# A graph network's fourth pass: scaling the node states on ScalarE instead of VectorE

## The chip, the cores and the metric

The kernel runs on one core of a Trainium2 chip. The metric is device time in microseconds for one launch, taken as the median of the runs shown. A core has five engines with an instruction stream each, which meet only at semaphores: TensorE (PE in the profile: matmuls and transposes), VectorE (DVE), ScalarE (ACT), GpSimd (POOL, which issues the indirect DMAs here) and SyncE (SP, which issues the plain ones). An engine takes its own instructions strictly in the order in which they were written.

## The reference

The network has 3125 nodes with 128 features and 100000 edges, sorted by destination. Four layers follow each other (a mean layer, three attention layers as one, a PNA layer, a SAGE layer), each after a layer norm. The change touches the end of the PNA layer only:

```python
msg = concat([node_feat[src], node_feat[dst]]) @ M_w.T + M_b
denom = maximum(deg, 1.0)[:, None]
mean = segment_sum(msg, dst) / denom
has_edge = (deg > 0)[:, None]
mx = where(has_edge, segment_max(msg, dst), 0.0)
mn = where(has_edge, segment_min(msg, dst), 0.0)
sq_mean = segment_sum(msg * msg, dst) / denom
std = sqrt(maximum(sq_mean - mean * mean, 0.0) + 1e-30)
h = concat([mean, mx, mn, std])
h = concat([h, h * amp, h * att])
h = (concat([node_feat, h]) @ U_w.T + U_b) * (1 / sqrt(n))
x = x + batch_norm(h)
```

Since `msg` is a part that depends on the source plus a part that depends on the destination, the kernel sums the source part alone and adds the destination's part (called `root`) to the mean, the largest and the smallest once for each node. The deviation does not need it.

## The kernel before

The 3125 nodes are 25 tiles of 128 nodes (`NT = 25`), the nodes on partitions and the features along the free dimension. At the end of a pass they are taken in five batches of five tiles (`NB = 5`, `BT = 5`).

The edges are walked in four passes, three for the attention layers and the fourth for PNA (`p.kind == PNA`). Each of 128 lanes walks 784 edges and stores a running state for every edge to DRAM (`rows`). For PNA that state has four blocks of 128 features: the sum of squares, the sum, the largest, and the largest of the negated values (so minus the smallest). After the last edge GpSimd fetches for each of the 25 tiles the state at each node's last edge (L645, one indirect DMA a tile) into `ends(p)`, which is a part of the large buffer `big`, as most tensors here.

Then come the steps that the change is about.

- **Node states.** A node whose edges begin in an earlier lane needs that lane's state. TensorE fetches it with a one-hot matmul for each tile (L1111, `psY<-Z,pick`, 128x512, f32, two banks in turn). VectorE's `node_states(b)` combines it: an add for the two sums (L1685) and a max for the two others (L1686), which raises `node_rdy`. TensorE's matmul of tile t waits for VectorE to have read tile t-2.
- **Layer out.** VectorE's `layer_out(b)` works on a whole batch, 128 x 640 elements for one block: the squares and the sum times `hrec` (one over the degree, or 0), the two largest times `has` (1 or 0), the mean squared into `mean_sq`, the subtraction, the max with 0 (L1730, raises `sd_in`), and `root` added to the three other blocks (L1731 to L1733, the last raises `agg_rdy`; the negated one turns over its sign there). That is ten instructions, L1724 to L1733.
- VectorE's order is `node_states(0)`, `node_states(1)`, `layer_out(0)`, `node_states(2)`, `layer_out(1)` and so on, then `layer_out(3)`, `layer_out(4)`.
- **ScalarE** takes the square root of a batch (L884, raises `sd_rdy`) and then copies the transposed tiles of that batch from PSUM (L889).
- **The product with U.** Once all 25 tiles have been combined, TensorE transposes four blocks of tile t (L1130, needs `agg_rdy` and `sd_rdy` of its batch), waits for ScalarE's copy (L889, `aggT_rdy`), and multiplies (L1141, eight instructions of 128x384 in the trace for a tile). Its order is: transposes of tile t, product of tile t-1, then two small matmuls that sum tile t-3 over the nodes (L1121). VectorE reads each product with three instructions (L1746 to L1748, raises `pna_rdy`); the product of tile t needs tile t-2 to have been read.

After the product come the batch norm, the layer norm, and the SAGE layer with dense adjacency counts (L934), which ends the kernel. TensorE works there almost without a gap.

Of the kernel before, what the change touches and what calls it, by code (L numbers as in the profile page):

```python
# [5 lines left out]
ALU = mybir.AluOpType  # L6
ACT = mybir.ActivationFunctionType
# [78 lines left out]
def build(nc, x, src, dst, W0, b0, Ws, Wd, att_s, att_d, gat_b, M_w, M_b, U_w, U_b, gamma, beta,  # L86
# [37 lines left out]
    with ExitStack() as ctx:  # L124
        def sb(name, shape, dt=F32):
            return ctx.enter_context(nc.sbuf_tensor(name, shape, dt))
# [4 lines left out]
        def sem(name):  # L131
            return ctx.enter_context(nc.semaphore(name))
# [42 lines left out]
        last = sb("last_s", [P, NT])  # L175
        has = sb("has", [P, NT])
        nohas = sb("nohas", [P, NT])
        hrec = sb("hrec", [P, NT])
# [122 lines left out]
        aggT = ring[:, NT * 4 * D:NT * 4 * D + 8 * P].rearrange("p (a w) -> p a w", a=2)  # L301
        mean_sq = ring[:, NT * 4 * D + 8 * P:NT * 4 * D + 8 * P + BT * D].rearrange("p (t d) -> p t d", d=D)
        rest = ring[:, NT * (TW + D):NT * (2 * TW + D)].rearrange("p (t w) -> p t w", w=TW)
        assert NT * (2 * TW + D) <= GMAX and NT * 4 * D + 8 * P + BT * D <= SIDE and NT * 4 * D <= ABUF

# [76 lines left out]
        sd_in, sd_rdy = sem("sd_in"), sem("sd_rdy")  # L382
        agg_rdy = sem("agg_rdy")
        aggT_ps, aggT_rdy = sem("aggT_ps"), sem("aggT_rdy")
# [266 lines left out]
        def _(act):  # L651
# [78 lines left out]
            for p in passes:  # L730
# [137 lines left out]
                if p.kind == GAT:  # L868
# [7 lines left out]
                    if g == 2:  # L876
                        deviations(2)
                        normalize(2)
                else:
                    for t in range(NT):  # L880
                        if t % BT == 0:
                            at = slice(t, t + BT)
                            act.wait_ge(sd_in, t // BT + 1)
                            nc.scalar.activation(ends(p)[:, at, 0:D], ends(p)[:, at, 0:D], ACT.Sqrt,  # L884
                                                 bias=eps[:, 1:2]).then_inc(sd_rdy, 1)
                        act.wait_ge(aggT_ps, t + 1)
                        if t >= 2:
                            act.wait_ge(pna_ps, t - 1)
                        nc.scalar.copy(aggT[:, t % 2, :], psT[t % 2][:]).then_inc(aggT_rdy, 1)  # L889
# [294 lines left out]
        def _(dve):  # L1184
# [270 lines left out]
            link(v.tensor_scalar(att[:], att[:], PNA_DELTA, None, ALU.mult))  # L1455
            link(v.tensor_scalar(amp[:], amp[:], 1.0 / PNA_DELTA, None, ALU.mult))
            dve.wait_ge(cross_ps, 1)
            link(v.tensor_scalar(cbias[:], psH[:, 0:NT], -1.0, BIG, ALU.add, ALU.mult))

            for p in passes:  # L1460
# [239 lines left out]
                def layer_out(b):  # L1700
# [21 lines left out]
                    else:  # L1722
                        sq, sm_, mx, nm = (e[:, :, k * D:(k + 1) * D] for k in range(4))
                        v.tensor_tensor(sq, sq, over_feats(hrec[:, at]), ALU.mult)  # L1724
                        link(v.tensor_tensor(sm_, sm_, over_feats(hrec[:, at]), ALU.mult))
                        v.tensor_tensor(mx, mx, over_feats(has[:, at]), ALU.mult)
                        link(v.tensor_tensor(mean_sq, sm_, sm_, ALU.mult))
                        v.tensor_tensor(nm, nm, over_feats(has[:, at]), ALU.mult)
                        link(v.tensor_tensor(sq, sq, mean_sq, ALU.subtract))
                        v.tensor_scalar(sq, sq, 0.0, None, ALU.max).then_inc(sd_in, 1)  # L1730
                        v.tensor_tensor(sm_, sm_, r_, ALU.add)  # L1731
                        link(v.tensor_tensor(mx, mx, r_, ALU.add))
                        v.tensor_tensor(nm, r_, nm, ALU.subtract).then_inc(agg_rdy, 1)  # L1733

# [68 lines left out]
```

## Time and profile before

| What | Value |
|---|---|
| median of 3 runs | 5279.04 us (5275.83 to 5281.31) |
| the profiled execution's own time | 5277.98 us |
| its span | 5275.9 us |
| node states and layer out of the fourth pass | 4765.0 to 4833.9 us |
| the product with U | its first tile at 4820.1, its last at 4908.7 us |
| SAGE layer's dense stage (L934) | from 4956.0 us to the end |

The profile is one execution. A row of the view of lines groups instructions of one form: busy time in total and the mean length of one, then the idle time of the engine just before them and what ended it. Busy time counts overlapped pieces once, so busy time divided by the count is the pace at which such instructions follow each other, and can be shorter than the mean length of one. A row of the timeline is one instruction or several merged ones: start, length, engine, line, the tiles; in brackets how long the engine had been idle and who ended that. A start and a length are in microseconds. The stretches' view gives busy time of each engine and the clock that TensorE was granted, where 1.00 is full speed, 2.4 GHz, and 0.50 is 1.2 GHz.

### The profile page before, as it was taken

What the parts mean: (1) busy time and instruction counts of PE and PEld (TensorE: products, weight loads), DVE (VectorE), ACT (ScalarE), POOL (GpSimd) and SP (SyncE); (2) the same over time, 40 slices, a digit from 0 to 9 for tenths busy, and PEclk for the clock granted to TensorE, in tenths of its full rate; (3) what the DMA queues carried; (4) which work ended last, traced back from release to release, by engine and by line L of the source; (5) the groups of instructions that cost most, each with busy time, mean ns of one, the idle gap of its engine ahead of it and who ended that gap; (6) DMA issues with size and microseconds to landing.
All of it is one profiled execution on the core that took longest, in us unless ns stands there. A gap on an engine that the chain in (4) does not pass through costs nothing.

```text
span 5275.9 us, 65740 instructions
## 1 busy us (share of the span) xinstructions
PE 3320.8 (63%) x13965; PEld 1555.5 (29%) x13965; DVE 4374.3 (83%) x14057; ACT 3173.8 (60%) x10162; POOL 3130.6 (59%) x3140
## 2 busy tenths in 40 slices
PE   4555578677777657777764777777343433336799
PEld 1111134333333233333322333333221111113444
DVE  7999989699999869999996999999788888885211
ACT  5666610677777557777764777777377777770100
POOL 3444400677777677777776777777377777771000
PEclk9999997788988778888886989898767667678899
DMA  4333362344444434444442444444267777772466
GB/s 140 131 131 131 131 246 95 86 128 128 127 122 129 120 82 129 127 123 127 129 123 68 128 129 129 123 126 129 60 244 278 281 280 282 280 279 64 177 234 224
DMA packets 324085, 817.57 MB, mean 155 GB/s; under 512 B 71032, under 2 KB 238948, under 8 KB 308904
## 3 DMA queue, kind: packets, MB, share of 16 engines
q1 hardware_dynamic: 225336, 605.05, 31.1%
q0 software_dynamic: 95024, 206.12, 16.4%
q10 hardware_dynamic: 3392, 2.75, 0.2%
q8 instruction: 112, 1.84, 0.1%
q14 instruction: 221, 1.81, 0.1%
HBM read 352.28 MB, written 461.40 MB: 154 GB/s over the span
## 4 chain that ended last, share of the span: by engine, by line
DVE 33%; POOL 18%; issue 11%; PE 11%; ACT 8%; DMA 6%; POOLq 0%; DVEq 0%; SPq 0%; ACTq 0%
POOL big L631 17%; DVE big L1606 8%; DVE big L1523 7%; PE psT L934 6%; DMA big<-table,src_win 4%; DVE big L1596 4%; DVE big L1546 2%; ACT hT L792 2%; DVE big L1616 2%; PE psY L1141 1%; DVE lane_x L1374 1%; DMA big<-A_d 1%; POOL big L645 1%; ACT hT L798 1%; ACT hT L807 1%
## 5 line engine op out<-in xcount | busy, mean ns | idle before, releaser
L631 POOL DMA_INDIRECT big<-table,src_win x2744 | 2647.8, 965 | 894.6 <-issue 798.6
L1054 PE MATMUL psY<-big,hT 128*128 128x420 bf16 x4200 | 1080.6, 405 | 725.0 <-ACT hT L798 724.1
L792 ACT ACTIVATE hT<-src_bc,node_c 128x128 bf16<-128x128 f16 x4200 | 1289.9, 386 | 63.2 <-DMA src_bc<-pe_src_d 54.2
L1606 DVE SCALAR_TENSOR_TENSOR big<-big,keep_win 128x132 f32<-128x132 f32 x2184 | 782.4, 358 | 77.8
L1054 PEld LDWEIGHTS psY<-big,hT 128*128 128x128 bf16 x4200 | 408.2, 110 | 1388.1 <-ACT hT L798 618.2
L1523 DVE TENSOR_SCALAR big<-src_bc,node_c 128x128 bf16<-128x128 f16 x4200 | 714.0, 284 | 0.6 <-issue 0.5
L1082 PE MATMUL psS<-big,hT 128*128 128x384 bf16 x1400 | 353.1, 430 | 549.4 <-DVE hT L1533 549.4
L798 ACT ACTIVATE hT<-hT 128x640 bf16<-128x640 bf16 x840 | 589.3, 720 | 0.0
L590 POOL TENSOR_SCALAR big<-big 128x400 bf16<-128x400 f16 x198 | 285.1, 1440 | 356.6 <-PE psY L993 166.8
L823 ACT ACTIVATE psH<-d_b 128x60 f32<-128x60 f32 x168 | 37.6, 224 | 695.2 <-DVE d_b L1588 695.2
L1060 PE MATMUL psL<-big 128*128 128x420 bf16 x2100 | 395.0, 344 | 18.1 <-DVE big L1523 15.6
L1060 PE MATMUL psZ<-big 128*128 128x420 bf16 x2100 | 390.0, 341 | 7.9 <-DVE big L1523 5.9
L1082 PEld LDWEIGHTS psS<-big,hT 128*128 128x128 bf16 x1400 | 170.3, 124 | 732.0 <-issue 694.1
L1596 DVE TENSOR_TENSOR big<-big,psH 128x1848 f32<-128x1848 f32 x168 | 349.4, 2080 | 26.2 <-ACT psH L823 22.1
L718 ACT ACTIVATE big<-big 128x400 bf16<-128x400 bf16 x396 | 212.3, 536 | 201.0 <-PE psY L993 99.4
L689 ACT COPY big<-psT 128x512 f32<-128x512 f32 (+1 forms) x21 | 11.3, 540 | 500.3 <-PE psT L934 500.3
L1295 DVE TENSOR_SCALAR big<-big 128x400 bf16<-128x400 f16 x990 | 306.8, 356 | 0.0
L934 PE MATMUL psT<-big 128*128 128x512 f32 (+1 forms) x700 | 281.2, 564 | 19.4 <-DMA big<-A_d 18.8
L1060 PEld LDWEIGHTS psL<-big 128*128 128x128 bf16 x2100 | 202.6, 98 | 208.3 <-DVE big L1523 37.6
L993 PE MATMUL psY<-big 128*128 128x400 bf16 x792 | 169.5, 337 | 144.0 <-DVE big L1295 144.0
L1060 PEld LDWEIGHTS psZ<-big 128*128 128x128 bf16 x2100 | 200.6, 98 | 195.4 <-DVE big L1523 29.6
L604 POOL DMA_INDIRECT start_ad<-big,start_i x75 | 81.2, 1082 | 282.3 <-ACT big L741 265.2
(327 smaller groups left out, 5381.8 us busy)
## 6 DMA issues: line engine op xcount, KB each, us to landing
rows<-big SPq DMA_DIRECT2D x112, 1792.0 KB
rows<-big SPq DMA_DIRECT2D x168, 952.0 KB
big<-A_d SPq DMA_DIRECT2D x18, 6400.0 KB, 19.8
A_d<-big SPq DMA_DIRECT2D x396, 200.0 KB, 1.9
big<-table,src_win POOLq DMA_INDIRECT x2744
src_bc<-pe_src_d SPq DMA_DIRECT2D x168, 64.0 KB
table<-big SPq DMA_DIRECT2D x15, 350.0 KB
big<-A_d SPq DMA_DIRECT2D x3, 1600.0 KB, 6.9
```

Of the source, the lines that this page charges most:

```text
L590: pool.tensor_scalar(hot_q[:, t % HOTS, GJ - 2, :], iota_q, qT[:, GJ - 2, t:t + 1], None, ALU.is_equal).then_inc(hot_p, 1)
L631: pool.indirect_dma_start(out=rows[:, k, 0:p.table_w], out_offset=None, in_=table, in_offset=bass.IndirectOffsetOnAxis(ap=src_win[:, s, k: ...
L792: ins = nc.scalar.activation(is_src[:, t, P:P + n], src_bc[:, s % 2, P:P + n], ACT.Square, bias=node_c[:, t:t + 1], scale=-1.0)
L798: nc.scalar.activation(is_src[:, at, 0:n], is_src[:, at, P:P + n], ACT.Relu, bias=1.0, scale=-1.0).then_inc(is_src_rdy, 1)
L934: ins = nc.tensor.matmul(psT[at % 2][:, 0:n * W].rearrange("f (b w) -> f b w", w=W), rows[:, s, :], abuf[(at + 1) % 2][:, 0:n, W * s:W * s ...
L1054: ins = nc.tensor.matmul(psF[0][s % 2][:, 0:3 * p.table_w], is_src[:, t, 0:P], table_s[:, t, :, :].rearrange("p c w -> p (c w)"), start=(t ...
L1060: ins = nc.tensor.matmul(psF[1][s % 2][:, 0:3 * p.table_w], is_src_v[s % 2][:, t, :], table_s[:, t, :, :].rearrange("p c w -> p (c w)"), s ...
L1082: ins = nc.tensor.matmul(psS[:, 0:3 * D].rearrange("p (c w) -> p c w", c=3), is_src[:, t, 0:P], table_s[:, t, :, 0:D], start=(n == 0), sto ...
L1295: ins = v.tensor_scalar(hot_q[:, t % HOTS, j, :], iota_q, qT[:, j, t:t + 1], None, ALU.is_equal)
L1523: ins = v.tensor_scalar(is_src_v[s % 2][:, t, :], src_bc[:, s % 2, 0:P], node_c[:, t:t + 1], None, ALU.is_equal)
L1596: v.tensor_tensor(for_heads, for_heads, over_heads(by_edge(cw_p[:, :, 1:15]), HC), ALU.mult).then_inc(chained, 1)
L1606: v.scalar_tensor_tensor(state[:, k, 0:GATW], prev[k][:, 0:GATW], kw[:, 0, k:k + 1], rows[:, k, 0:GATW], ALU.mult, ALU.add).then_inc(chain ...
```

## The change

ScalarE's stream at the end of the fourth pass gets the scaling. For each tile, as soon as VectorE has combined it, it multiplies the largest by `has`, the negated smallest by `minus` (a new tensor, minus `has`, so that the sign is turned here), and writes the square of the sum times `hrec` to `mean_sq`, of which there are now two buffers. After five tiles it multiplies the squares and the sum of each tile by `hrec` in one instruction of 128x256 in place, and raises `scaled`. Then it takes the square root of the batch before. VectorE's `layer_out` keeps three instructions: the subtraction, the max, and one add of `root` to the three other blocks at once (128 x 5 x 384). It waits for `scaled` first. The copies of the transposed tiles now come after all five square roots.

```diff
@@ ScalarE, end of the fourth pass
+                    en = ends(p)
+                    for b in range(NB + 1):
+                        for t in range(BT * b, min(BT * (b + 1), NT)):
+                            act.wait_ge(node_rdy, NT * p.number + t + 1)
+                            if t % BT == 0 and b >= 2:
+                                act.wait_ge(sd_in, b - 1)
+                            nc.scalar.mul(en[:, t, 2 * D:3 * D], en[:, t, 2 * D:3 * D], has[:, t:t + 1])
+                            nc.scalar.mul(en[:, t, 3 * D:4 * D], en[:, t, 3 * D:4 * D], minus[:, t:t + 1])
+                            nc.scalar.activation(mean_sq[b % 2][:, t % BT, :], en[:, t, D:2 * D], ACT.Square,
+                                                 scale=hrec[:, t:t + 1]).then_inc(squared, 1)
+                        if b < NB:
+                            act.wait_ge(squared, BT * (b + 1))
+                            for t in range(BT * b, BT * (b + 1)):
+                                ins = nc.scalar.mul(en[:, t, 0:2 * D], en[:, t, 0:2 * D], hrec[:, t:t + 1])
+                            ins.then_inc(scaled, 1)
+                        if b:
+                            at = slice(BT * (b - 1), BT * b)
+                            act.wait_ge(sd_in, b)
+                            nc.scalar.activation(en[:, at, 0:D], en[:, at, 0:D], ACT.Sqrt,
+                                                 bias=eps[:, 1:2]).then_inc(sd_rdy, 1)
                     for t in range(NT):
-                        if t % BT == 0:
-                            at = slice(t, t + BT)
-                            act.wait_ge(sd_in, t // BT + 1)
-                            nc.scalar.activation(ends(p)[:, at, 0:D], ends(p)[:, at, 0:D], ACT.Sqrt,
-                                                 bias=eps[:, 1:2]).then_inc(sd_rdy, 1)
                         act.wait_ge(aggT_ps, t + 1)
@@ VectorE, before the passes
+            link(v.tensor_scalar(minus[:], has[:], -1.0, None, ALU.mult))
@@ VectorE, layer_out
-                        sq, sm_, mx, nm = (e[:, :, k * D:(k + 1) * D] for k in range(4))
-                        v.tensor_tensor(sq, sq, over_feats(hrec[:, at]), ALU.mult)
-                        link(v.tensor_tensor(sm_, sm_, over_feats(hrec[:, at]), ALU.mult))
-                        v.tensor_tensor(mx, mx, over_feats(has[:, at]), ALU.mult)
-                        link(v.tensor_tensor(mean_sq, sm_, sm_, ALU.mult))
-                        v.tensor_tensor(nm, nm, over_feats(has[:, at]), ALU.mult)
-                        link(v.tensor_tensor(sq, sq, mean_sq, ALU.subtract))
+                        dve.wait_ge(scaled, b + 1)
+                        sq = e[:, :, 0:D]
+                        link(v.tensor_tensor(sq, sq, mean_sq[b % 2], ALU.subtract))
                         v.tensor_scalar(sq, sq, 0.0, None, ALU.max).then_inc(sd_in, 1)
-                        v.tensor_tensor(sm_, sm_, r_, ALU.add)
-                        link(v.tensor_tensor(mx, mx, r_, ALU.add))
-                        v.tensor_tensor(nm, r_, nm, ALU.subtract).then_inc(agg_rdy, 1)
+                        others = e[:, :, D:4 * D].rearrange("p t (k d) -> p t k d", d=D)
+                        v.tensor_tensor(others, others, r_.unsqueeze(2).broadcast_to([P, BT, 3, D]), ALU.add).then_inc(agg_rdy, 1)
```

VectorE's stream before, from the last tile of `node_states(1)` over `layer_out(0)` to the first tile of `node_states(2)`:

```order
L1686 SCALAR_TENSOR_TENSOR big<-psY,cbias,big 128x256
L1724 TENSOR_TENSOR big<-big,hrec 128x5x128 [waits node_rdy]
L1725 TENSOR_TENSOR big<-big,hrec 128x5x128
L1726 TENSOR_TENSOR big<-big,has 128x5x128 [waits dve_chain]
L1727 TENSOR_TENSOR big<-big 128x640
L1728 TENSOR_TENSOR big<-big,has 128x5x128 [waits dve_chain]
L1729 TENSOR_TENSOR big<-big 128x5x128
L1730 TENSOR_SCALAR big<-big 128x5x128 [waits dve_chain]
L1731 TENSOR_TENSOR big<-big 128x5x128
L1732 TENSOR_TENSOR big<-big 128x5x128
L1733 TENSOR_TENSOR big<-big 128x5x128 [waits dve_chain]
L1685 TENSOR_TENSOR big<-psY,big 128x256 [waits node_ps,ends_in2]
```

VectorE's stream of the change, the same `layer_out(0)` between the same neighbours:

```order
L1744 TENSOR_TENSOR big<-big 128x5x128 [waits scaled,node_rdy]
L1745 TENSOR_SCALAR big<-big 128x5x128 [waits dve_chain]
L1747 TENSOR_TENSOR big<-big 128x5x384
```

Seven of ten instructions are gone, and the first that is left waits for ScalarE.

ScalarE's stream before, from the last edge of the pass on:

```order
L839 ACTIVATE psH<-big 128x128
L884 ACTIVATE big<-big,eps 128x5x128 [waits sd_in]
L889 COPY big<-psT 128x512 [waits aggT_ps] x2
L889 COPY big<-psT 128x512 [waits pna_ps,aggT_ps] x3
L884 ACTIVATE big<-big,eps 128x5x128 [waits sd_in]
```

ScalarE's stream of the change in the middle of it: the last square of a batch, its five scalings, the square root of the batch before, and the next batch's first tile:

```order
L890 ACTIVATE big<-big,hrec 128x128
L895 ACTIVATE big<-big,hrec 128x256 [waits squared]
L895 ACTIVATE big<-big,hrec 128x256 x4
L900 ACTIVATE big<-big,eps 128x5x128 [waits sd_in]
L888 ACTIVATE big<-big,has 128x128 [waits sd_in,node_rdy]
L889 ACTIVATE big<-big,minus 128x128
```

And at its end, where both last square roots stand ahead of the first copy of a transposed tile:

```order
L895 ACTIVATE big<-big,hrec 128x256 x4
L900 ACTIVATE big<-big,eps 128x5x128 [waits sd_in] x2
L906 COPY big<-psT 128x512 [waits aggT_ps] x2
L906 COPY big<-psT 128x512 [waits pna_ps,aggT_ps] x23
```

ScalarE's first copy has moved from behind the first square root to behind the fifth. TensorE's stream is the same in both.

## Rows read from the trace of the kernel before

**Rows 1.** The page, part 1: busy time, share of the span, instructions of each engine.

```profile
PE 3320.8 (63%) x13965; PEld 1555.5 (29%) x13965; DVE 4374.3 (83%) x14057; ACT 3173.8 (60%) x10162; POOL 3130.6 (59%) x3140
```

**Rows 2.** Timeline, VectorE and ScalarE in the first layer out of the fourth pass.

```profile
4776.45 0.85 DVE L1724 TENSOR_TENSOR big<-big,hrec 128x640 f32<-128x640 f32 x1
...
4780.41 0.82 DVE L1729 TENSOR_TENSOR big<-big 128x640 f32<-128x640 f32 x1
...
4781.74 0.81 DVE L1731 TENSOR_TENSOR big<-big 128x640 f32<-128x640 f32 x1
4781.85 0.83 ACT L884 ACTIVATE big<-big,eps 128x640 f32<-128x640 f32 x1 [34.11 <-DVE big L1730]
...
4783.31 0.82 DVE L1733 TENSOR_TENSOR big<-big 128x640 f32<-128x640 f32 x1
...
4784.06 0.42 DVE L1685 TENSOR_TENSOR big<-psY,big 128x256 f32<-128x256 f32 x1
```

**Rows 3.** Timeline, node states of the second batch: VectorE's tiles 5 and 7, TensorE's last.

```profile
4771.53 0.42 DVE L1685 TENSOR_TENSOR big<-psY,big 128x256 f32<-128x256 f32 x1 [0.46 <-PE psY L1111]
...
4773.57 0.42 DVE L1685 TENSOR_TENSOR big<-psY,big 128x256 f32<-128x256 f32 x1 [0.46 <-PE psY L1111]
...
4776.47 0.30 PEld L1111 LDWEIGHTS psY<-Z,pick 128*128 128x128 f32 x2 [0.88 <-DVE big L1686]
```

**Rows 4.** Timeline, node states of the third and fifth batch, and TensorE's restart.

```profile
4784.92 7.08 PE L1111 MATMUL psY<-Z,pick 128*128 128x512 f32 x10 [7.32 <-DVE big L1686]
...
4790.85 0.82 DVE L1724 TENSOR_TENSOR big<-big,hrec 128x640 f32<-128x640 f32 x1
...
4812.45 0.42 DVE L1685 TENSOR_TENSOR big<-psY,big 128x256 f32<-128x256 f32 x1
...
4818.71 0.83 DVE L1724 TENSOR_TENSOR big<-big,hrec 128x640 f32<-128x640 f32 x1
```

**Rows 5.** Stretches: busy PE, PEld, DVE, ACT, POOL, TensorE's clock, DMA share, GB/s.

```profile
4770.00:4777.00 7.00, 6.70 (x14) 2.16 (x14) 5.60 (x14) 0.00 (x0) 5.28 (x6) 1.00 0.71 211
...
4785.00:4790.00 5.00, 5.00 (x7) 2.09 (x8) 2.22 (x6) 0.00 (x0) 2.84 (x3) 0.56 0.65 188
```

**Rows 6.** Timeline, the beginning of the product with U.

```profile
4818.73 1.09 PE L1130 MATMUL psT<-ident,big 128*128 128x128 f32 x8 [0.91 <-DVE big L1686]
...
4823.18 2.75 PE L1141 MATMUL psY<-wT,big 128*128 128x384 f32 x8
4823.38 0.59 ACT L889 COPY big<-psT 128x512 f32<-128x512 f32 x1 [2.89 <-PE psT L1130]
...
4834.98 5.49 PE L1141 MATMUL psY<-wT,big 128*128 128x384 f32 x8 [8.61 <-DVE big L1748]
...
4841.08 2.75 PE L1141 MATMUL psY<-wT,big 128*128 128x384 f32 x8
...
4844.32 2.75 PE L1141 MATMUL psY<-wT,big 128*128 128x384 f32 x8
```

**Rows 7.** Lines by form, ScalarE: busy us, mean ns of one, idle before.

```profile
L792 ACT ACTIVATE hT<-src_bc,node_c 128x128 bf16<-128x128 f16 x4200 | 1289.9, 386 | 63.2 <-DMA src_bc<-pe_src_d 54.2 <-PE psY L1054 9.0
...
L662 ACT ACTIVATE big<-xt,shift,rstd 128x128 f32<-128x128 f32 x100 | 38.9, 479 | 0.0
...
L884 ACT ACTIVATE big<-big,eps 128x640 f32<-128x640 f32 x5 | 4.1, 830 | 34.1 <-DVE big L1730 34.1
```

**Rows 8.** The page, part 5: VectorE's long multiplication with a broadcast operand.

```profile
L1596 DVE TENSOR_TENSOR big<-big,psH 128x1848 f32<-128x1848 f32 x168 | 349.4, 2080 | 26.2 <-ACT psH L823 22.1
```

**Rows 9.** Timeline of TensorE: one form (128x512, f32) after a shorter and a longer gap.

```profile
786.42 2.05 PE L1012 MATMUL psL<-sm,ones 128*128 128x512 f32 x2 [4.09 <-DVE tmp L1390]
...
856.23 1.10 PE L1012 MATMUL psL<-sm,ones 128*128 128x512 f32 x2 [3.38 <-DVE tmp L1390]
```

**Rows 10.** Timeline: GpSimd's last fetch of end rows that the timeline lists.

```profile
4787.76 0.94 POOL L645 DMA_INDIRECT big<-rows,end_i  x1 [0.30 <-issue]
```

**Rows 11.** Timeline: VectorE before the passes, the wait behind `minus`.

```profile
933.35 0.18 DVE L1458 TENSOR_SCALAR cbias<-psH 128x25 f32<-128x25 f32 x1 [5.06 <-PE psH L1025]
```

More of the change, by code:

```diff
@@ L176, in build @@
         has = sb("has", [P, NT])
+        minus = sb("minus", [P, NT])
         nohas = sb("nohas", [P, NT])
@@ L301, in build @@
         aggT = ring[:, NT * 4 * D:NT * 4 * D + 8 * P].rearrange("p (a w) -> p a w", a=2)
-        mean_sq = ring[:, NT * 4 * D + 8 * P:NT * 4 * D + 8 * P + BT * D].rearrange("p (t d) -> p t d", d=D)
+        mean_sq = [ring[:, NT * 4 * D + 8 * P + z * BT * D:NT * 4 * D + 8 * P + (z + 1) * BT * D].rearrange("p (t d) -> p t d", d=D)
+                   for z in range(2)]
         rest = ring[:, NT * (TW + D):NT * (2 * TW + D)].rearrange("p (t w) -> p t w", w=TW)
-        assert NT * (2 * TW + D) <= GMAX and NT * 4 * D + 8 * P + BT * D <= SIDE and NT * 4 * D <= ABUF
+        assert NT * (2 * TW + D) <= GMAX and NT * 4 * D + 8 * P + 2 * BT * D <= SIDE and NT * 4 * D <= ABUF
         def ends(p):
@@ L382, in build @@
         sd_in, sd_rdy = sem("sd_in"), sem("sd_rdy")
-        agg_rdy = sem("agg_rdy")
+        squared, scaled, agg_rdy = sem("squared"), sem("scaled"), sem("agg_rdy")
         aggT_ps, aggT_rdy = sem("aggT_ps"), sem("aggT_rdy")
```

## The prediction

> **What bounds the kernel now.** The page's first part comes first, and only as a warning: VectorE is busy for 83% of the span and ScalarE for 60% [rows 1], but the change touches only some 70 us of 5276, so those shares say nothing. What counts is which wait ends last between the node states (4765) and the fourth tile of the product with U. Behind that the steps hang on each other as before, and I carry a shift there to the end.
>
> The timeline of that stretch shows three parts. A layer out takes VectorE 7.61 us, from 4776.45 to 4784.06 [rows 2], and ScalarE has done nothing for 34 us when the first square root comes. The node states are a ping-pong of VectorE and TensorE. At the full clock two tiles take 2.04 us (4771.53 to 4773.57) [rows 3], but after each layer out TensorE has been idle for 7.3 us and restarts at a granted clock near one half (0.56, against 1.00 in the second batch) [rows 4, 5]. Such a batch takes 6.79 us (4784.06 to 4790.85) or 6.26 us (4812.45 to 4818.71) [rows 2, 4]. The product with U starts at 4818.7, gets two tiles done, and then stands for 8.6 us until VectorE has finished its last two layer outs. From its third tile (4834.98, at half clock, 6.10 us to the next) it is bound by TensorE at 3.24 us a tile [rows 6]. So VectorE's layer outs are on the path, all but the first two tiles' worth of the last two, and TensorE's cold restarts with them.
>
> **VectorE's part.** The subtraction and the max stay: 4780.41 to 4781.74, 1.33 us [rows 2]. The new add has 1920 elements. The 640-element one takes 0.82 us [rows 2] and a 1848-element one with a broadcast operand 2.08 us [rows 8], so 1.04 ns an element, and the new one 2.08 + 72 x 1.04 ns = 2.16 us, some 0.07 of it under the next instruction. A layer out becomes 1.33 + 2.16 - 0.07, with a little for the wait 3.45 us, a saving of 4.16. No row has this exact pattern (one operand repeated over a middle dimension, in place). Below: nothing shows an f32 add faster than this. Above: half the rate, 4.3 us, a rival below.
>
> **ScalarE's part.** For each batch it gets 15 instructions of 128x128 with one operand that is a value per partition, 5 of 128x256, and the square root as before. The nearest row is L792, the same shape with one such operand: 1289.9 us by 4200 is 0.307 us apart, 0.386 for one alone. L884 has 640 elements and takes 0.830, so 0.87 ns an element more, and the 256-wide one comes every 0.307 + 0.11 = 0.42 us. L662, with two such operands, comes every 0.389 [rows 7]. The squares and products here have one, so I take 0.307 and keep 0.389 for the range. A batch is 15 x 0.307 + 5 x 0.42 + 0.83 + about 0.2 for two waits = 7.7 us. Downwards it gains nothing, since VectorE needs 3.45 + 4.9 = 8.35 us a batch (below). ScalarE had been idle there, so this costs nothing as long as `scaled` is up in time. Behind each wait on ScalarE stands only its own work, and for `scaled` of batch b VectorE comes a whole batch later, except in the last. There the last tile's three instructions end 1 us after the node states, the scalings 2.2 us later, and `scaled` is up at +3.2 us, just before VectorE has done layer out 3 at +3.45.
>
> The Trainium skill speaks against the edit here: the rules for kernel authors in "ScalarE: Activation LUTs" say to multiply on VectorE, not ScalarE. By that rule each scaling costs more than it did, and it is true for one instruction; it would decide only if ScalarE were the later of the two. The same page's section "What ACT_TABLE_LOAD costs" puts an ACTIVATE with one per-partition operand at 280 ns + 0.833 ns an element and the overlap at 93 ns, an estimate of 0.294 us for 128 elements. The trace agrees within 13 ns (0.307), and by the page the batch would be some 0.3 us shorter and the sum the same. Neither stream has a table load in this stretch.
>
> **The clock.** With 3.45 us of layer out TensorE is idle for only 3.45 + 0.80 - 1.1 = 3.15 us between batches (its last matmul starts as VectorE's layer out does, at 4776.47 [rows 3]). The trace has one form after both kinds of gap: after 3.38 us it took 1.10 us, after 4.09 us 2.05 us [rows 9]. 3.15 lies on the fast side, so I take the full clock for the third to fifth batch. Five tiles at 1.02 are 5.1 us, and since the first two wait for nothing, 4.9.
>
> **The sum.** The first two batches of node states come before any layer out and stay. Three batches then take 3 x (3.45 + 4.9) = 25.05 us from 4776.45 and end at 4801.5 instead of 4818.7. That is 17.2 us, 12.5 from the layer outs and 4.7 from the clock (the three took 42.26 - 3 x 7.61 = 19.4 us, now 14.7). The last end rows are fetched from 4787.76 on [rows 10], and the fifth batch needs them at 4796.6: not a new bound.
>
> Now the end is worse than before. ScalarE's first copy of a transposed tile stands behind the fifth square root, so the product's first tile waits for layer out 3 (3.45), subtraction and max of layer out 4 up to the root's start (4780.41 to 4781.85, 1.44 [rows 2]), the root 0.83, the copy 0.59 and handovers 0.1: 6.4 us, at 4807.9. TensorE has by then been idle for some 5.2 us, so this tile runs at half clock: 5.9 us to the next (6.10 before, less two small matmuls), then 3.1 and 3.24. The fourth tile starts at 4807.9 + 12.2 = 4820.1, where it started at 4841.08 [rows 6]. **That is 21.0 us.** VectorE ends layer out 4 before it is wanted for the third tile. `minus` costs nothing: VectorE waits for TensorE for 5.06 us behind it [rows 11]; without that cover it would be 0.2 us. Nothing else is moved past a DMA issue. The profiled execution's 5277.98 becomes 5257.0; the median lies 1.06 above it, so 5258.0.
>
> **Rivals.**
> - *Half clock between the batches after all.* If the short bursts don't keep the clock up, the 4.7 us stay: 16.3 us gained, 5262.7. The row at 4.09 us speaks for it, the one at 3.38 against.
> - *The product's first tile at full clock.* Then 2.8 us more: 5255. Its gap of 5.2 us speaks against.
> - *ScalarE sets the pace.* At 0.389 apart (0.50 for the wide ones) the work of a batch up to `scaled` is 8.4 us and the root 0.93. It starts at about 4765.9 and loses 1 us at TensorE's slow first tiles, so the last `scaled` is at 4766.9 + 5 x 8.4 + 3 x 0.93 = 4811.7, the product's first tile 3.0 later, the fourth at 4826.9: 14 us gained, 5265.
> - *The threefold add at half rate.* Layer out 5.6 us; TensorE's gaps are then past 4.09 us. 4 x 2.1 more in the layer outs and 4.7 from the clock, 13 of 21 gone: 8 us gained, 5271. The row of 1848 elements speaks against.
> - *Slower.* ScalarE's instructions, in place on the rows that VectorE has just written, each take so long that `scaled` is late throughout. Equality is where the last `scaled` comes at 4825.9, that is 11.2 us a batch without the root, or 0.53 us for a 128x128 instruction (20 of them and 0.65 for the width). At 0.60 the last `scaled` is at 4832.9 and the fourth tile at 4848.1: 5286. Against it: even two operands and no overlap at all are 0.479 [rows 7], which still gains some 5 us.
> - *It doesn't do what it says.* Here it must: the ten instructions are three in VectorE's stream.
>
> **How the numbers follow.** Forecast 0.50, product's first tile at full clock 0.07, half clock between batches 0.16, ScalarE's pace 0.13, half-rate add 0.05, slower 0.04, and 0.05 for a gain under 10.6 us from something I don't see, such as the later stages giving some back. About 0.2%, 10.6 us, is what a measurement can tell from no change. Faster: 0.50 + 0.07 + 0.16 + 0.13 = 0.86. Same: 0.05 + 0.05 = 0.10. Slower: 0.04. The range takes in the first four, 5255 to 5265, with 3 us either side for the spread of the runs: 5252 to 5268.
>
> **What would show it.** In the changed kernel's timeline: layer outs of 3.4 us without a wait ahead of the subtraction, except perhaps the last; TensorE's idle time between batches near 3.1 us and batches of 4.9 us after it; ScalarE's group of 75 instructions 0.31 us apart; the last node state near 4801.5; the product's first tile near 4808 and its fourth near 4820, both counted from the same start of the stretch. A wait of VectorE for ScalarE of more than 1 us in each batch would mean the third rival, an add of over 3 us the fourth. The prediction would be wrong as a whole if the fourth tile gained 21 us and the end did not: then what I took as rigid behind the product is not.

## The result and the profile after

The changed kernel takes 5257.99 us (median of 6 runs, 5253.67 to 5262.09). The kernel before took 5277.07 beside it (6 runs, 5274.55 to 5281.31). The ratio is 0.9963, with a 95% interval of 0.9951 to 0.9975: **faster by 0.37%, some 19 us**, where 5258.0 was forecast. The profiled execution took 5255.98 us, its span is 5253.9. In some of the sets of runs below, a part of the executions of every kernel, the one before included, is over 1.5% longer than its fastest: medians are of all executions, each ratio is of the others only, so a ratio need not be the quotient of the two medians.

The first part of the page answers to [rows 1]: VectorE has 34 instructions fewer and 21 us less to do, ScalarE 100 more.

```profile
PE 3315.6 (63%) x13965; PEld 1554.4 (30%) x13965; DVE 4353.5 (83%) x14023; ACT 3207.0 (61%) x10262; POOL 3130.4 (60%) x3140
```

The timeline of VectorE in the first layer out, against [rows 2] (start, length, engine, line, tiles; in brackets the idle time before and who ended it). From the subtraction to the next node state it is 4773.91 to 4777.31, 3.40 us where it was 7.61, and no wait stands ahead of the subtraction.

```profile
4773.91 0.83 DVE L1744 TENSOR_TENSOR big<-big 128x640 f32<-128x640 f32 x1
4774.77 0.56 DVE L1745 TENSOR_SCALAR big<-big 128x640 f32<-128x640 f32 x1
4775.25 2.14 DVE L1747 TENSOR_TENSOR big<-big 128x1920 f32<-128x1920 f32 x1
4777.31 0.42 DVE L1703 TENSOR_TENSOR big<-psY,big 128x256 f32<-128x256 f32 x1
...
4780.29 0.42 DVE L1703 TENSOR_TENSOR big<-psY,big 128x256 f32<-128x256 f32 x1 [1.44 <-PE psY L1128]
...
4783.41 0.82 DVE L1744 TENSOR_TENSOR big<-big 128x640 f32<-128x640 f32 x1
```

TensorE's timeline, against [rows 4, 6]: the restarts after each layer out, and the first tiles of the product with U. Its idle time ahead of a batch is 3.11 us where it was 7.32.

```profile
4778.17 6.39 PE L1128 MATMUL psY<-Z,pick 128*128 128x512 f32 x10 [3.11 <-DVE big L1704]
4787.67 6.58 PE L1128 MATMUL psY<-Z,pick 128*128 128x512 f32 x10 [3.11 <-DVE big L1704]
4797.36 4.54 PE L1128 MATMUL psY<-Z,pick 128*128 128x512 f32 x6 [3.11 <-DVE big L1704]
4802.81 1.10 PE L1147 MATMUL psT<-ident,big 128*128 128x128 f32 x8 [0.91 <-DVE big L1704]
4808.98 4.31 PE L1158 MATMUL psY<-wT,big 128*128 128x384 f32 x8 [5.07 <-ACT big L906]
...
4813.56 2.75 PE L1158 MATMUL psY<-wT,big 128*128 128x384 f32 x8
...
4816.58 2.75 PE L1158 MATMUL psY<-wT,big 128*128 128x384 f32 x8
...
4819.82 2.75 PE L1158 MATMUL psY<-wT,big 128*128 128x384 f32 x8
```

The view of stretches, against [rows 5]: busy PE, PEld, DVE, ACT, POOL, then TensorE's granted clock. The first row is TensorE's burst, the second its gap, the third and fourth its restart in the third batch. The last two are the gap and the restart of the fourth batch.

```profile
4769.40:4775.06 5.66, 5.66 (x12) 1.49 (x10) 4.79 (x12) 5.63 (x18) 4.39 (x5) 1.00 0.73 214
4775.06:4778.17 3.11, 0.00 (x1) 0.00 (x0) 3.11 (x5) 3.08 (x10) 2.81 (x2) 0.95 0.58 169
4778.17:4780.29 2.12, 2.12 (x3) 1.09 (x4) 0.68 (x3) 2.12 (x6) 1.51 (x3) 0.50 0.52 131
4780.29:4781.70 1.41, 1.41 (x3) 0.50 (x3) 0.81 (x2) 1.27 (x5) 1.10 (x2) 0.66 0.76 192
...
4784.56:4787.67 3.11, 0.00 (x1) 0.00 (x1) 3.11 (x5) 2.74 (x7) 2.81 (x2) 1.00 0.44 137
4787.67:4789.80 2.13, 2.13 (x3) 0.92 (x4) 1.04 (x4) 1.84 (x6) 0.04 (x1) 0.60 0.39 123
```

So the clock is not kept: each of the three batches has a stretch at half clock near its start and is at 1.00 again before it ends. In the third the clock fell just before the matmuls started again. In the fourth it was still 1.00 through the gap, and fell after they had.

**Where the time went.** I measure the stretch from the first node state to the start of the product's fourth tile, where the prediction's sum ends. Before it is 4765.04 to 4841.08, 76.04 us. After it is 4761.91 to 4819.82, 57.91 us.

| Piece of the stretch | before | after | gain |
|---|---|---|---|
| node states, first two batches | 11.41 | 12.00 | -0.6 |
| layer outs 0 to 2 | 22.77 | 10.19 | 12.6 |
| node states, batches 3 to 5 | 19.49 | 18.68 | 0.8 |
| last node state to the product's fourth tile | 22.37 | 17.04 | 5.3 |
| together | 76.04 | 57.91 | 18.1 |

A batch is counted from VectorE's first instruction on it to the subtraction behind it. The three of the changed kernel are 6.10, 6.29 and 6.29 us long; the last ends at 4802.78. The dense stage of the SAGE layer starts at 4934.7 us instead of 4956.0, 21.3 us earlier. The missing 3.1 us lie ahead of the stretch, which began 3.1 us earlier in this execution, though nothing there was changed. In the traces of one chip (after_again, only_add, fill, early) its start lies anywhere from 4756.2 to 4764.4 us, so this is spread and no gain.

### The profile page after: what moved, and what is told of

Its sections match the earlier page's. It is cut to its first block, busy times and chain, and to the rows that moved or that the text cites. A ratio compares the mean times of both kernels' runs of the same rounds, so it can differ in the third digit from the quotient of the medians.

```text
span 5253.9 us, 65813 instructions
## 1 busy us (share of the span) xinstructions
PE 3315.6 (63%) x13965; PEld 1554.4 (30%) x13965; DVE 4353.5 (83%) x14023; ACT 3207.0 (61%) x10262; POOL 3130.4 (60%) x3140
## 3 DMA queue, kind: packets, MB, share of 16 engines
q8 instruction: 112, 1.84, 0.1%
## 4 chain that ended last, share of the span: by engine, by line
DVE 33%; POOL 19%; issue 11%; PE 11%; ACT 6%; DMA 5%; POOLq 0%; DVEq 0%; SPq 0%; ACTq 0%
POOL big L633 18%; DVE big L1624 8%; DVE big L1541 8%; PE psT L951 6%; DVE big L1614 4%; DMA big<-table,src_win 3%; DVE big L1634 2%; DVE big L1564 2%; PE psY L1158 1%; POOL big L647 1%; ACT hT L794 1%; DVE lane_x L1391 1%; ACT hT L809 1%; DMA big<-A_d 1%; DVE hT L1551 1%
```

## The experiments

Four kernels ran on one chip (after_again, only_add, fill and early; the kernel before took 5274.15 us beside them). On the three chips that the other eight runs got, every kernel, the one before included, took 6.7 to 6.8 ms. Their traces show pauses of several us whose end the trace puts on no engine of the kernel. Their totals compare only with their own runs of before. From their traces I use the pieces that no pause touches, and say where one does.

**The change once more.**

> The changed kernel as it is, beside the others on one chip. The gain in the stretch between the first node state and the fourth tile of the product with U should be 18 us again (it was 41.08 - 4765.04 against 4819.82 - 4761.91). The other 3 us of the first trace lay ahead of the stretch, in passes that the change doesn't touch. If they are spread of the gathers, the start of the node states differs from trace to trace by a few us either way, and the median gain lies between 17 and 20 us. If the change moves something in the passes, it is some 3 us early again.

5254.43 us (5 runs, 5248.09 to 5257.98), ratio 0.9961 (0.9947 to 0.9974). The stretch is 57.53 us, within 0.4 of the first, and the same 3.11 us gaps with the same half clock behind them.

**One add instead of three, and the multiplications left on VectorE.** In the kernel before, `minus` replaces `has` for the last part and the three adds of the root part become one:

```diff
-                        v.tensor_tensor(nm, nm, over_feats(has[:, at]), ALU.mult)
+                        v.tensor_tensor(nm, nm, over_feats(minus[:, at]), ALU.mult)
...
-                        v.tensor_tensor(sm_, sm_, r_, ALU.add)
-                        link(v.tensor_tensor(mx, mx, r_, ALU.add))
-                        v.tensor_tensor(nm, r_, nm, ALU.subtract).then_inc(agg_rdy, 1)
+                        others = e[:, :, D:4 * D].rearrange("p t (k d) -> p t k d", d=D)
+                        v.tensor_tensor(others, others, r_.unsqueeze(2).broadcast_to([P, BT, 3, D]), ALU.add).then_inc(agg_rdy, 1)
```

> The kernel before with one part of the change alone: VectorE turns the sign of the negated smallest with its scaling and adds root to three blocks in one instruction. ScalarE gets nothing. Theory (what pays is the seven instructions' worth of work that left VectorE): a layer out goes from 7.61 us to 7.61 - (3 x 0.8) + 2.1 = 7.4 us, so 5 x 0.2 = 1 us in all, 5276, not to be told from no change. Rival (the single add is itself what pays, by fewer starts and waits): half of the 12.6 us of the layer outs or more, 5268 or below.

5271.97 us (11 runs, 5267.71 to 5277.91), ratio 0.9998 (0.9989 to 1.0007), and a stretch of 75.78 us. Its timeline of VectorE, the fourth layer out:

```profile
4811.34 0.83 DVE L1726 TENSOR_TENSOR big<-big,hrec 128x640 f32<-128x640 f32 x1
...
4816.60 2.14 DVE L1734 TENSOR_TENSOR big<-big 128x1920 f32<-128x1920 f32 x1
4818.66 0.82 DVE L1726 TENSOR_TENSOR big<-big,hrec 128x640 f32<-128x640 f32 x1
```

A layer out is 7.32 us instead of 7.61: the long add costs 2.06 us where the three short ones cost 2.32 (4781.74 to 4784.06 in [rows 2]). So of the 4.2 us that a layer out lost in the change, some 0.3 are the single add's and 3.9 are work that left VectorE.

**TensorE kept busy between the batches (the clock).** Matmuls that nobody reads, which follow the second one of a batch: 6 in each of the third to fifth batch and 10 ahead of the product's first tile, later 3 and 5. Each is two in the trace:

```diff
+                    if p.kind == PNA:
+                        for _ in range({1: 0, 11: 6, 16: 6, 21: 6}.get(t, 0)):
+                            nc.tensor.matmul(psL[:], ident[:], Z[:], start=True, stop=True)
...
+                            for _ in range(10 if t == 1 else 0):
+                                nc.tensor.matmul(psL[:], ident[:], Z[:], start=True, stop=True)
```

> The changed kernel with filler matmuls (128x512, f32, into a bank that nobody reads) in TensorE's gaps: six behind the matmul of tiles 11, 16 and 21, and ten between the second tile's transposes and the product's first tile. The forecast took the full clock for the third to fifth batch, and the trace shows they took 6.1 to 6.3 us at a granted clock near 0.7. Theory (it is the clock that makes these batches longer than 4.9): with the gaps filled they take 4.9 us, 4 us less in all, and the product's first tile 3.1 us instead of 4.6, so 5.5 us faster than the change. Rival (the handover between VectorE and TensorE sets 6.2 us, whatever the clock): no gain, or a loss of up to 2 us where a filler delays a matmul that is wanted.

5257.19 us (6 runs, 5254.07 to 5258.2), ratio 0.9968 (0.9956 to 0.998), stretch 60.87 us: slower by 3 us than the change, which the fill was not to be. TensorE's timeline, and the third batch in the view of stretches:

```profile
4769.44 5.31 PE L1132 MATMUL psL<-Z,ident 128*128 128x512 f32 x12
4774.59 5.09 PE L1128 MATMUL psY<-Z,pick 128*128 128x512 f32 x10
...
4799.64 8.75 PE L1154 MATMUL psL<-Z,ident 128*128 128x512 f32 x20
4808.22 2.74 PE L1163 MATMUL psY<-wT,big 128*128 128x384 f32 x8
```

```profile
4771.80:4778.50 6.70, 6.65 (x15) 2.31 (x13) 4.03 (x11) 5.60 (x17) 5.18 (x6) 1.00 0.57 169
```

The clock stayed at 1.00, and yet the batches took 6.7 us. The filler was too long: the batch's next matmul was wanted at 4772.71 and began at 4774.59, and the product's first tile came 9.54 us behind the last node state instead of 6.2. What it gave (that tile's 4.58 us to the next became 3.02) was less than the 3.3 us that its own filler cost. Half as much filler was therefore the next run.

> The changed kernel with half the filler of the run called fill: three (six matmuls in the trace, 2.6 us) in each of the three gaps of 3.1 us, five (4.3 us) in the gap of 5.1 us before the product's first tile. The longer filler held the granted clock at 1.00 but delayed the matmul that VectorE waits for by 1.9 us a batch and the product's first tile by 3.4. Theory (the clock is what makes a batch of node states 6.2 us): the batches take 4.9 us and the product's first tile 3.1, so the stretch from the first node state to the product's fourth tile is 57.7 - 4 - 1.5 = 52.2 us. Rival (handover, not clock): the batches stay above 6 us and the stretch above 56.

> The kernel of the run called fill_short again, for the same reason (one pause of 9.1 us in its stretch). Its undisturbed batches took 4.88 us. Theory: the third to fifth batch 4.9 us each and the stretch 52.2 to 53 us, against 57.7 in the change. Rival (the filler also delays): above 55 us.

6748.1 us (10 runs, 6704.57 to 6784.23), ratio 0.996 (0.9927 to 0.9992), and on another chip 6781.36 (14 runs, 6696.1 to 6917.27), 0.9987 (0.9952 to 1.0022). The stretches are 62.21 and 62.24 us, both with a pause in the third batch. In the first it stands ahead of one node state. VectorE's timeline, that row and the untouched fifth batch:

```profile
6290.85 0.42 DVE L1708 TENSOR_TENSOR big<-psY,big 128x256 f32<-128x256 f32 x1 [9.11 <-remote]
...
6306.68 0.42 DVE L1708 TENSOR_TENSOR big<-psY,big 128x256 f32<-128x256 f32 x1
...
6308.71 0.42 DVE L1708 TENSOR_TENSOR big<-psY,big 128x256 f32<-128x256 f32 x1 [0.49 <-PE psY L1128]
...
6311.59 0.82 DVE L1749 TENSOR_TENSOR big<-big 128x640 f32<-128x640 f32 x1
```

6306.68 to 6311.59 is 4.91 us, where the change took 6.29. The fifth batch of the other run is 4.92, and the product's first tile comes 6.2 us behind the last node state, as in the change, and takes 3.12 to the next. Without the 9.11 us the first stretch would be 53.1. Put together from undisturbed pieces of that trace (11.61 for the first two batches, three layer outs of 3.40, three batches of 4.91, 15.58 from the last node state on) it would be 52.1, against an expected 52.2. Both are arithmetic. The mechanism is shown, the total is not: neither chip gives a time for the kernel that compares with 5254.

**The product's first tiles copied earlier.** ScalarE's first two copies of transposed tiles (`aggT_copy(t)` is the copy of tile t with its waits) move: the first goes ahead of the last five scalings, the second behind them and ahead of the last two square roots:

```diff
+                        if b == NB - 1:
+                            aggT_copy(0)
                         if b < NB:
                             act.wait_ge(squared, BT * (b + 1))
                             for t in range(BT * b, BT * (b + 1)):
                                 ins = nc.scalar.mul(en[:, t, 0:2 * D], en[:, t, 0:2 * D], hrec[:, t:t + 1])
                             ins.then_inc(scaled, 1)
+                        if b == NB - 1:
+                            aggT_copy(1)
...
-                    for t in range(NT):
+                    for t in range(2, NT):
```

> The changed kernel with ScalarE's first two copies of transposed tiles moved: the first ahead of the last batch's five scalings, the second behind them, both ahead of the last two square roots. Theory: the product's first tile waits for nothing but ScalarE's copy, so it starts about 1.8 us after the last node state instead of 6.2, VectorE ends its last layer out 0.5 us later, and the third tile starts when VectorE has read the first, about 8.3 us after the last node state instead of 13.8. That is 5 us faster than the change. Rival (VectorE's last layer outs bind the third tile anyway): under 1 us.

**5245.58 us** (5 runs, 5240.27 to 5255.36), ratio 0.9945 (0.9931 to 0.9958). It is the best of the kernels whose totals compare, 8.9 us under the change and 28.6 under before in that comparison. The stretch is 52.55 us, 5.0 to 5.4 less than the change's two. From the first node state to the dense stage of the SAGE layer it is 168.7 us where the change's two take 172.8 and 172.4, so in this trace some 4 us of the 5 arrive there. The rest went in the batch norm, where the same 50 matmuls took 8.90 us instead of 7.67; in early_again they took 6.04 and in only_add 8.99, so that is spread. That the medians differ by 9 is more than the traces show, and the runs of the two kernels overlap. Its timeline at the product's start:

```profile
4805.60 1.09 PE L1155 MATMUL psT<-ident,big 128*128 128x128 f32 x8 [0.91 <-DVE big L1712]
...
4806.47 0.56 ACT L888 COPY big<-psT 128x512 f32<-128x512 f32 x1
...
4807.09 2.85 PE L1166 MATMUL psY<-wT,big 128*128 128x384 f32 x8 [0.40 <-ACT big L888]
...
4810.21 2.75 PE L1166 MATMUL psY<-wT,big 128*128 128x384 f32 x8
...
4813.58 2.85 PE L1166 MATMUL psY<-wT,big 128*128 128x384 f32 x8 [0.19 <-DVE big L1770]
```

The first tile comes 1.5 us behind the last node state instead of 6.2. TensorE had waited 0.40 us and not 5.07, so it also runs at full clock, 3.12 us to the next instead of 4.58. A wait of 0.19 us ahead of the third tile is all that appears in its place: VectorE reads the product's first tile (L1770) only when its last layer out is done.

> The kernel of the run called early again, to compare with the run beside it. Its stretch should be 52.6 us again, 23.5 less than in the kernel before, and its median 23 us under that of the kernel before (the first time it was 28.6 under, more than the stretch explains, with runs 15 us apart).

6815.41 us on a chip with pauses (12 runs, 6694.69 to 6934.71), ratio 1.001 (0.9955 to 1.0064): nothing can be told from that total. Its stretch is 57.64 us and not the 52.6 expected, with pauses in the third batch, which took 12.0 us. Its trace repeats the 1.5 us at the product's start and gives the counterpart for the next kernel.

**Both at once:** the early copies, 6 filler matmuls behind the first batch's second one and 3 between the others.

> The changed kernel with the two early copies of the run called early, three fillers in each of the three gaps of 3.1 us, and six behind the first two matmuls of the node states, where TensorE waits 7.6 us for VectorE. If the two gains add: the stretch from the first node state to the product's fourth tile is 52.6 (early) less 4 for the three batches and up to 1 for the first two: 48 us, against 76 before, and the median 28 us under the kernel before. If they don't add, because ScalarE (7.7 us a batch) then comes late for VectorE (8.3 us a batch), it is 50 to 52, with waits of VectorE for ScalarE ahead of its subtractions.

> The kernel of the run called both again, because the chip of its first run ran every kernel at 6.7 ms and its trace has pauses inside the stretch in which no engine that was waited for was late (4.1 and some 6 us). With the pauses taken off, its stretch from the first node state to the product's fourth tile was about 48.6 us. Theory: 48 to 49 us here, which is 27 to 28 us less than the kernel before (76), and the median 27 us less than its median. Rival (ScalarE comes late when the batches are 8.3 us): 50 to 52 us, 25 us less.

> The kernel of the run called both, beside early on the same chip. Fourth and fifth batch of node states took 4.87 us in both earlier runs, where a pause of 4 us and more lay in the second or third. Theory: without a pause the stretch from the first node state to the product's fourth tile is 48 to 49 us (52.6 in early, 57.7 in the change, 76 before), and the median lies 4 us under that of early. Rival: 50 to 52 us and at most 2 us under early.

6749.83 us, ratio 0.9964 (11 runs, interval 0.9936 to 0.9992); 6783.53, 1.0001 (12 runs, 0.9952 to 1.0051); 6764.44, 0.9963 (13 runs, 0.9921 to 1.0005). The stretches of 58.58, 59.21 and 57.43 us all hold pauses. The pauses of the first are about 10 us, which would leave some 48.6, against 48 to 49 expected. Undisturbed pieces of both_third and both (11.34 for the first two batches, three layer outs of 3.39, three batches of 4.91, 11.34 from the last node state on) add up to 47.6. Both are arithmetic, no measured time. What is measured is the batches, 4.91 or 4.92 us each wherever no pause fell. The fifth batch on the same chip, with the filler (both_third, first two fences) and without (early_again, last two), each as TensorE's restart in the timeline, and under it the batch in the view of stretches:

```profile
6452.95 3.16 PE L1136 MATMUL psY<-Z,pick 128*128 128x512 f32 x6 [0.54 <-DVE big L1715]
```

```profile
6452.10:6457.00 4.90, 3.43 (x7) 0.97 (x6) 3.97 (x11) 4.17 (x13) 0.00 (x0) 1.00 0.00 0
```

```profile
6273.49 4.54 PE L1136 MATMUL psY<-Z,pick 128*128 128x512 f32 x6 [3.11 <-DVE big L1712]
```

```profile
6272.70:6278.90 6.20, 4.54 (x6) 1.54 (x6) 3.91 (x11) 4.22 (x13) 0.00 (x0) 0.72 0.00 0
```

VectorE and ScalarE do the same work in both. TensorE's gap is 0.54 us or 3.11, the granted clock 1.00 or 0.72, and the batch 4.92 or 6.29 us. The 1.4 us between them are the clock's.

**More work for ScalarE,** to find where its pace begins to count: 25 more squares that nobody reads, or 75.

```diff
+                            for x in range(1):
+                                nc.scalar.activation(spare[:, 5 * x + t % BT, :], en[:, t, D:2 * D], ACT.Square,
+                                                     scale=hrec[:, t:t + 1])
```

> The changed kernel with one more square for each tile on ScalarE, into a buffer that nobody reads: 25 instructions, 1.5 us a batch. Theory (ScalarE has slack in all batches but the last; VectorE's batch is 9.5 us, ScalarE's 7.7 and now 9.3): the stretch grows from 57.7 us by under 1.5 us, all of it as one wait ahead of the last subtraction. Rival (ScalarE's pace already sets the batches): by 1.5 us a batch, 7 us.

6746.39 us (10 runs, 6723.04 to 6807.01), ratio 0.996 (0.9929 to 0.9992). The stretch is 61.28 us, 3.4 to 3.8 more than the change's two, where under 1.5 was expected. ScalarE's square roots and VectorE's last subtraction, from the timeline:

```profile
6338.31 0.82 ACT L904 ACTIVATE big<-big,eps 128x640 f32<-128x640 f32 x1
6347.01 0.81 ACT L904 ACTIVATE big<-big,eps 128x640 f32<-128x640 f32 x1
...
6355.83 0.82 DVE L1748 TENSOR_TENSOR big<-big 128x640 f32<-128x640 f32 x1 [2.15 <-ACT big L899]
```

ScalarE needs 8.70 us a batch and VectorE 9.69, so ScalarE should always have been ahead. But the first two batches of node states come with no layer out between them, and ScalarE falls behind there. It then makes up only 1 us a batch, and VectorE waits 2.15 us for it ahead of the last subtraction. But 1.78 us of this wait are a pause of ScalarE in the third batch: from there to the last scaling it stood idle nowhere, so the pause went through to the end whole, and some 0.4 us is left for the backlog. The product's first tile comes later and, after a longer gap, takes 5.32 us to the next where it was 4.58. Without the pause the stretch would be 1.6 to 2.0 us longer than the change's, by arithmetic, near the 1.5 that was expected.

> The same with three more squares for each tile, 4.6 us a batch, which makes 11.4 us of ScalarE's work for a batch without its root (12.3 with it), above VectorE's 9.5. It tests the price at which the prediction's slower case was to decide: 11.2 us a batch without the root. Theory: ScalarE now works without a pause and VectorE waits ahead of every subtraction; the last one comes some 17 us later than in the change, so the stretch is 73 to 77 us, where the kernel before has 76. Rival (VectorE's batches hide part of it): under 68 us.

6783.91 us (10 runs, 6751.23 to 6807.35), ratio 1.0007 (0.998 to 1.0033) against the same runs of before: the gain of the change, 0.4%, is gone. VectorE's timeline in this kernel, two of its five subtractions:

```profile
6313.66 0.83 DVE L1748 TENSOR_TENSOR big<-big 128x640 f32<-128x640 f32 x1 [1.84 <-ACT big L899]
...
6325.27 0.83 DVE L1748 TENSOR_TENSOR big<-big 128x640 f32<-128x640 f32 x1 [1.01 <-ACT big L899]
```

VectorE waits for ScalarE ahead of four subtractions, 4.96, 1.84, 1.01 and 8.06 us, and the batches follow each other every 11.6 us, ScalarE's pace. The stretch is 80.72 us; without the 7.3 us of ScalarE's pauses it would be near 73, at the lower end of the expected 73 to 77. Here ScalarE needs 10.9 us a batch without the root, and the prediction's point of equality was 11.2.

## Why the prediction was right, and where it was not

- **Layer out, 7.61 to 3.45 us: right.** It is 3.40, and three of them gave 12.6 us, forecast 12.5. The add of 1920 elements takes 2143 ns, forecast 2.16 us. The rival at half rate is refuted.
- **ScalarE's part costs nothing: right, its price a little high.** The new instructions follow each other every 0.292 us, forecast 0.307, and the wide ones every 0.42, as forecast. The Trainium skill's "ScalarE: Activation LUTs", section "What ACT_TABLE_LOAD costs", gave an estimate of 0.294, and these rows agree with it better than the one at 0.307 did. The rule of the same page of the Trainium skill ("Rules for kernel authors") to multiply on VectorE is no guide here: VectorE was the later of the two, and moving the work took some 11.8 of the 12.6 us from its three layer outs, the single add the rest (only_add). VectorE waits for no scaling in the two traces of the change. act_one_more and act_three_more show that this cover was real and about how large: with 25 instructions more some 0.4 us of a wait appear at the last subtraction, with 75 more VectorE waits at four of five. The first two batches, which have no layer out between them, use up more of it than the sum a batch says. The rival on ScalarE's pace had this start in it; the forecast's "VectorE needs 8.35 us a batch" had not.
- **Full clock in batches 3 to 5, 4.7 us: this step failed.** 0.8 us came. The gap was foretold well (3.11 us, forecast 3.15), and what it does was not: in the 13 gaps of 3.11 us that no pause touches (three each in after, after_again, early and act_one_more, one in early_again) the clock fell every time, from 0.5 us before the matmuls started again to 1.1 us behind. The step took [rows 9] for a sign that 3.38 us of idling leave the clock up. It was a misreading: the two matmuls of that row ended just before the clock fell, and the next 2 us, in which TensorE was busy without a pause, had 0.50. The view is in the last section. So [rows 9] holds no row of a kept clock. The rival "half clock between the batches after all" is what happened in the batches. fill_short and both show that the clock is the cause: the same batches take 4.91 us when TensorE has something to do in the gap.
- **The product's first tile, 6.4 us behind the last node state: right.** It is 6.2, for the reason given: ScalarE's copy stands behind the fifth root. early shows it by taking that order away.
- **That tile at half clock, 5.9 us to the next: too high.** It took 4.58 and 4.53 in the two traces. The clock came back within the tile (0.50 from 4809.0 to 4811.9, 1.00 from 4812.0 on). The forecast took the row at 6.10 us before, where TensorE had been idle 8.61 us.
- **The first two batches stay: off by -0.6 us.** They took 12.0 instead of 11.41. Their first tiles run at half clock too, and how many differs from trace to trace: in the kernels that leave these two batches alone the second starts 6.5 to 7.4 us behind the first.
- **The sum, 21.0 us in the stretch: 18.1.** It came short by 3.9 in the clock and by 0.6 in the first batches, and 0.1 more came in the layer outs and 1.5 more at the end. That 5258.0 and 5257.99 agree so closely is luck: errors of both signs, and the kernel before came out at 5277.07 beside the change and not at 5279.04, 2 us lower than what the forecast started from. Of the 19.1 us between the medians the stretch explains 18.1. By its own terms, mended, the forecast would have been 5261. "The product's first tile at full clock" was refuted, "it doesn't do what it says" and "slower" as well. For the last, 10.9 us a batch still left the stretch, less the pauses, 3 us under before, which fits the 11.2 that was put as equality and does not measure it.

**What stays open.** What the kernel with early copies and filler takes on a chip without pauses: its three runs fell on chips with them. Why these chips pause, in all kernels alike. Why the median of early lies 4 to 5 us further down than its trace explains.

## What to carry to other kernels

When two engines take turns, price a move of work by what the turn gets shorter, then look at the first instruction behind the stretch: here a copy that stood behind unrelated work of the engine that had been given more cost over a quarter of what the change had brought, 5 us of 18. Count an engine's cover from where its backlog starts, not only by its work per period. A gap made shorter need not give back a clock: from 7.32 to 3.11 us it gave 0.8 of the 4.7 us that were forecast. A fast matmul right behind a gap does not show that the clock was kept; read the granted clock of the microseconds that follow as well. A little filler tells what the clock is worth, but a filler longer than the gap delays the work behind it.

## What the chip showed that was not expected

- **The clock can fall behind the gap, when TensorE is already busy again.** The row of [rows 9] with the shorter gap, in the kernel before, as burst, gap, its two matmuls and the 2 us that follow:

```profile
846.00:852.80 6.80, 6.80 (x16) 2.67 (x15) 6.80 (x1) 0.00 (x0) 0.00 (x0) 1.00 0.00 0
852.80:856.20 3.40, 0.05 (x1) 0.00 (x1) 3.26 (x7) 0.59 (x1) 0.00 (x0) 1.00 0.37 86
856.20:857.40 1.20, 1.17 (x5) 0.72 (x5) 1.13 (x3) 0.00 (x0) 0.00 (x0) 0.93 1.03 393
857.40:859.40 2.00, 2.00 (x10) 2.00 (x11) 1.13 (x5) 0.00 (x0) 0.00 (x0) 0.50 1.05 402
```

  The clock was 1.00 through the gap and 0.93 over the two matmuls, and 0.50 behind them. In the fourth batch of the change it was 1.00 through all 3.11 us of the gap and 0.60 over the 2.13 us that followed. So two gaps of one length can look different in the matmuls right behind them, although the clock falls in both.
- **Shorter gaps left it at 1.00:** 0.54 us (both_third's fifth batch), 0.9 us (early's product start) and, behind the filler of the first batch, 2.31 us in the run called both:

```profile
6268.97:6271.27 2.30, 0.00 (x0) 0.00 (x0) 0.87 (x3) 0.01 (x1) 1.69 (x3) 1.00 0.69 208
6271.27:6274.00 2.73, 2.67 (x6) 0.97 (x6) 2.19 (x6) 2.57 (x9) 2.11 (x3) 1.00 0.79 215
```

  What gap between 2.3 and 3.11 us is still short enough, no run here settles.
- **A chip can pause.** On three of the four chips that took experiments every kernel was some 28% longer (6.75 against 5.27 ms), with pauses of 1 to 10 us in single engines, whose end the trace puts on nothing that the kernel does.
